# A graph network's node stage in batches of ten tiles with lagged matmuls, and the ranking's products laid out by stream

## The reference

```python
h = relu(layernorm(x))
x = x + L0(h)      # relu(LN(segment_sum((h @ W_lin @ W_gcn)[src] * norm, dst) + b_gcn) * gamma + beta)
h = relu(layernorm(x))
x = x + L1(h, edge_attr_128, edge_attr_128_n2)
# L1, four heads of 32: q = h @ Wq + bq for nodes; k, v from the two edge arrays
# score = (q[src] . k) * scale; softmax over the edges of one src; out = segment_sum(attn * v, src) @ Wo + bo
```

## Time and profile before

| | |
|---|---|
| median of 3 runs | 4865.36 us (4861.69 to 4885.93) |
| the profiled execution | 4897.3 us, span 4895.6 us |
| busy: PE, DVE, ACT, POOL | 3389.2, 2855.3, 2454.4, 2047.4 us |
| mean granted TensorE clock | 0.771 |
| moved by DMA | 764.21 MB, 156 GB/s over the span |

### The profile page before, as it was taken

One profiled execution on the slowest core, in us unless ns is written; L12 is line 12 of the kernel. 1 busy time (PEld: TensorE's weight loads), 2 busy tenths in 40 slices (PEclk: granted clock), 3 DMA queues, 4 the chain that ended last, 5 costly groups with the idle time before them and its releaser, 6 DMA issues. The chain is left out here.

```text
span 4895.6 us, 79918 instructions
## 1 busy us (share of the span) xinstructions
PE 3389.2 (69%) x21299; PEld 2441.0 (50%) x21299; DVE 2855.3 (58%) x5810; ACT 2454.4 (50%) x7415; POOL 2047.4 (42%) x1890
## 2 busy tenths in 40 slices
PE   3488767778777774021454567666668998999898
PEld 2266544455554452011333455555556776777665
DVE  6877787888887673530000455555556777777611
ACT  0545598888898784010232334333334665666411
POOL 1677287777777777777001433333331000000000
PEclk7655579999998897555555788888888999999855
DMA  1554144444444545456211566666666666666400
GB/s 59 168 173 163 49 138 162 155 160 160 161 151 157 170 160 183 142 170 208 88 33 53 187 207 222 216 208 214 212 209 196 189 190 203 189 189 190 132 0 26
DMA packets 511558, 764.21 MB, mean 156 GB/s; under 512 B 53848, under 2 KB 377408, under 8 KB 511358
## 3 DMA queue, kind: packets, MB, share of 16 engines
q1 hardware_dynamic: 406798, 522.56, 35.2%
q0 software_dynamic: 78160, 226.14, 12.2%
q10 hardware_dynamic: 26400, 13.21, 0.9%
HBM read 515.95 MB, written 245.75 MB: 156 GB/s over the span
## 5 line engine op out<-in xcount | busy, mean ns | idle before, releaser
L550 POOL DMA_INDIRECT table_s<-ring,place x1612 | 1894.3, 1175 | 1158.0 <-DMA ring<-in_kv 576.0
L623 ACT ACTIVATE row_base<-row_base 128x196 f32<-128x196 f32 x1616 | 883.3, 557 | 200.2 <-DVE row_base L718 189.5
L1346 PE MATMUL bank<-kT,G 128*128 128x384 f32 x1200 | 573.3, 562 | 235.9 <-ACT kT L1393 139.4
L1393 ACT COPY kT<-bank 128x384 f32<-128x384 f32 x600 | 286.5, 477 | 595.3 <-remote 264.6
L1366 PE MATMUL bank<-kv_rows,exT 128*128 128x129 f32 x3600 | 536.1, 288 | 0.0
L943 PE MATMUL bank<-xres 128*128 128x98 bf16 x3136 | 315.3, 236 | 291.4 <-ACT work L662 192.2
L1437 DVE TENSOR_REDUCE gmax<-bank 128x1 f32<-128x384 f32 x600 | 333.2, 555 | 299.2 <-remote 116.7
L962 PE MATMUL bank<-parts,work 128*128 128x384 bf16 x2401 | 501.2, 367 | 0.0
L1366 PEld LDWEIGHTS bank<-kv_rows,exT 128*128 128x128 f32 x3600 | 486.7, 205 | 0.1
L662 ACT CAST work<-bank 128x392 bf16<-128x392 f32 x784 | 373.1, 510 | 165.4 <-PE bank L943 98.3
L1017 DVE SCALAR_TENSOR_TENSOR others<-kv_rows,node_s,iota_h 128x384 bf16<-128x384 f32 x600 | 371.4, 619 | 135.1 <-DMA kv_rows<-table_s 79.2
(11 more groups left out here) (272 smaller groups left out, 4915.5 us busy)
## 6 DMA issues: line engine op xcount, KB each, us to landing
kv_rows<-table_s SPq DMA_DIRECT2D x600, 408.0 KB, 3.1
ring<-in_kv SPq DMA_DIRECT2D x402, 512.0 KB
G<-G_dram SPq DMA_DIRECT2D x600, 64.5 KB, 2.7
table_s<-ring,place POOLq DMA_INDIRECT x1612
G_dram<-gst ACTq DMA_DIRECT2D x50, 258.0 KB
x_dram<-xres SPq DMA_DIRECT2D x1, 3200.0 KB, 15.2
out<-ring SPq DMA_DIRECT2D x1, 3072.0 KB
table_s<-parts SPq DMA_DIRECT2D x6, 136.0 KB, 3.8
```

The source lines that it names most:

```text
L550: pool.indirect_dma_start(out=m["table_s"], out_offset=bass.IndirectOffsetOnAxis(ap=m["place"][0:n, i, k:k + 1], axis=0), in_=m["ring"][0: ...
L623: last = nc.scalar.activation(at, at, ACT.Identity, accum_out=m["place_f"][:, i % 2, h * STREAMS // 2 + k:h * STREAMS // 2 + k + 1])
L1346: pe.matmul(scores[k][:, 0:SGE], m["G"][:, u, 0:P], m["kT"][:, k, :], start=False, stop=True, skip_group_check=True).then_inc(m["scored"], 1)
```

## The change

POOL_STEPS becomes (130, 144). `scatter_rows` copies the keys of the next step before it waits for this one's places. `products` is laid out as half, stream, tile, so that VectorE writes with a stride of 196 elements and ScalarE sums over neighbours. In the node stage the norm goes in five batches of ten tiles, each in eight stages; while a batch's tiles pass through the matmuls, the next batch's stages are done between them on VectorE. The four `qm` move from ScalarE to VectorE (with the bias added before the scale, so `qbias` is gone), `hs` from VectorE to ScalarE. TensorE does the transpose two tiles ahead and the Wq product one tile ahead. `gst` has four buffers; its store is issued one tile later. All loops of the stage are written out. `x` is loaded in three DMAs, the first ten tiles at once and without a wait, and stored in five. The diff, cut:

```diff
-POOL_STEPS = (132, 156)
+POOL_STEPS = (130, 144)
+BATCH_T, GSTS = 10, 4
...
 def scatter_rows(m, pool, i):
     u, first = i % KRING, STREAMS - columns(i)
-    need(pool, m["rows_sent"][u], sent_before(i))
-    pool.tensor_copy(m["ring"][:, u, first:STREAMS, KEY_AT:KEY_AT + 1], m["sources"][:, i, first:STREAMS].rearrange("p (s a) -> p s a", a=1)).then_inc(m["keys_ready"], 1)
+    for j in ((0, 1) if i == 0 else (i + 1,) if i + 1 < STEPS else ()):
+        v, at = j % KRING, STREAMS - columns(j)
+        need(pool, m["rows_sent"][v], sent_before(j))
+        pool.tensor_copy(m["ring"][:, v, at:STREAMS, KEY_AT:KEY_AT + 1], m["sources"][:, j, at:STREAMS].rearrange("p (s a) -> p s a", a=1)).then_inc(m["keys_ready"], 1)
     pool.wait_ge(m["places_ready"], i + 1)
...
-                        at = m["products"][:, h, :, k:k + 1].rearrange("p t a -> p (t a)")
+                        at = m["products"][:, h, k, :]
...
-                    dve.tensor_tensor(m["products"][:, h, :, :].rearrange("p (b t) s -> p b t s", b=RANK_BANKS),
+                    dve.tensor_tensor(m["products"][:, h, :, :].rearrange("p s (b t) -> p b t s", b=RANK_BANKS),
...
         def _(sp):
+            for k, (first, end) in enumerate(((0, BATCH_T), (BATCH_T, N // P))):
+                sp.dma_start(m["xres"][:, first:end, :], node_tiles(m["x"][first * P:end * P, :])).then_inc(m["x_again_loaded"][k], 16)
             sp.wait_ge(m["x_padded"], 1)
-            load_x(m, sp)
+            sp.dma_start(m["xres"][0:N % P, N // P, :], m["x"][N // P * P:N, :]).then_inc(m["x_again_loaded"][1], 16)
             for i in range(POOL_STEPS[0] + KRING, POOL_STEPS[1] + KRING):
                 load_rows(m, sp, i)
-            sp.wait_ge(m["x_ready"], 1)
-            sp.dma_start(node_tiles(m["x_dram"]), m["xres"][:, :, :]).then_inc(m["x_stored"], 16)
+            for b in range(NT // BATCH_T):
+                sp.wait_ge(m["x_ready"], b + 1)
+                sp.dma_start(node_tiles(m["x_dram"])[:, part(b), :], m["xres"][:, part(b), :]).then_inc(m["x_stored"], 16)
...
+            def queries(t):
+                u = t % 2
+                dve.wait_ge(m["q_summed"], t + 1)
+                need(dve, m["G_summed"], t - 1)
+                for h in range(HEADS):
+                    last = dve.tensor_scalar(m["qm"][:, u, :, h, :], m["bank"][2 + u][:, 0:P].rearrange("d (q n) -> d q n", q=PARTS),
+                                             m["w"]["bq"][:, 0:1], m["qscale"][:, h:h + 1], ALU.add, ALU.mult)
+                last.then_inc(m["q_ready"], 1)
+            for stage in range(8):
+                normal(0, stage)
+            for t in range(NT):
+                b, stage = t // BATCH_T + 1, t % BATCH_T
+                if b < NT // BATCH_T and stage < 8:
+                    normal(b, stage)
+                queries(t)
...
+            for t in range(NT):
+                b, stage = t // BATCH_T + 1, t % BATCH_T
+                if b < NT // BATCH_T and stage in (2, 6):
+                    root(b, stage // 4)
+                if t + 3 < NT:
+                    hidden(t + 3)
+                if t + 2 < NT:
+                    turned(t + 2)
+                if t > 0:
+                    stored(t - 1)
+                taken(t)
...
+            for t in range(NT):
+                if t + 2 < NT:
+                    turn(t + 2)
+                if t + 1 < NT:
+                    query(t + 1)
+                keyed(t)
```

More of the change, by code:

```diff
@@ L1182, in nodes_block, with part @@
 def nodes_block(nc, m):
+    def part(b):
+        return slice(b * BATCH_T, (b + 1) * BATCH_T)
     with nc.Block() as block:
@@ L1252, in _, with root, hidden @@
-            rounds(act, copies, 0, NT // 2, 2)
-            for u in range(2):
-                act.wait_ge(m["G_stored"][u], NT // 2 * 16)
+            def root(b, which):
+                act.wait_ge(m["sqrt_asked"], 2 + 2 * b + which)
+                nc.scalar.activation(m["std"][:, part(b)], m["var"][:, part(b)], ACT.Sqrt).then_inc(m["sqrt_done"], 1)
+            def hidden(t):
+                if t % BATCH_T == 0:
+                    act.wait_ge(m["norm_ready"], 3 + 2 * (t // BATCH_T))
+                need(act, m["h2_transposed"], t - 1)
+                nc.scalar.activation(m["hs"][:, t % 2, :], m["work"][:, t, :], ACT.Relu, scale=m["rstd"][:, t:t + 1]).then_inc(m["h2_ready"], 1)
@@ new lines, in stored @@
+            def stored(t):
+                act.wait_ge(m["G_ready"], t + 1)
+                act.dma_start(m["G_dram"][t * PARTS * P:(t + 1) * PARTS * P, :].rearrange("(q d) n -> d q n", q=PARTS),
+                              m["gst"][:, t % GSTS, :, :]).then_inc(m["G_stored"][t % GSTS], 16)
+            for which in range(2):
+                root(0, which)
+            hidden(0)
+            hidden(1)
+            turned(0)
+            hidden(2)
+            turned(1)
+            for t in range(NT):
[9 more added lines that the diff above has]
+                taken(t)
@@ L1256, in _, with turn @@
+            stored(NT - 1)
+            for v in range(GSTS):
+                act.wait_ge(m["G_stored"][v], len(range(v, NT, GSTS)) * 16)
         @block.tensor
         def _(pe):
-            def body(i, u, r):
-                pe.wait_ge(m["h2_ready"], i + 1)
-                need(pe, m["h2T_ready"], i - 1)
-                pe.transpose(m["bank"][u][:, 0:P], m["hs"][:, u, :], m["ident"][:, :]).then_inc(m["h2_transposed"], 1)
-                pe.wait_ge(m["h2T_ready"], i + 1)
-                need(pe, m["q_ready"], i - 1)
-                pe.matmul(m["bank"][2 + u][:, 0:P], m["w"]["Wq"][:, :], m["hT"][:, u, :], start=True, stop=True).then_inc(m["q_summed"], 1)
-                pe.wait_ge(m["q_ready"], i + 1)
-                need(pe, m["G_ready"], i - 1)
+            def turn(t):
+                pe.wait_ge(m["h2_ready"], t + 1)
+                need(pe, m["h2T_ready"], t - 1)
+                pe.transpose(m["bank"][t % 2][:, 0:P], m["hs"][:, t % 2, :], m["ident"][:, :]).then_inc(m["h2_transposed"], 1)
@@ L1271, in body @@
                 last.then_inc(m["G_summed"], 1)
-            rounds(pe, body, 0, NT // 2, 2)
+            turn(0)
+            turn(1)
+            query(0)
+            for t in range(NT):
[4 more added lines that the diff above has]
+                keyed(t)
 def layer1_block(nc, m):
@@ L1614, in gnn_kernel @@
             for name, shape, dt in (
-                    *((n, [P, NT], F32) for n in small), ("flags_i", [P, 1], I32), ("qscale", [P, HEADS], F32), ("qbias", [P, HEADS], F32),
+                    *((n, [P, NT], F32) for n in small), ("flags_i", [P, 1], I32), ("qscale", [P, HEADS], F32),
                     ("hs", [P, 2, D], F32), ("work", [P, NT, D], F32), ("acc", [P, NT, D], F32), ("xres", [P, NT, D], F32)):
@@ L1712, in gnn_kernel @@
                 general_block(nc, m)
-            for name, shape, dt in (("qm", [P, 2, PARTS, HEADS, SN], F32), ("gst", [P, 2, PARTS, P + 1], F32)):
+            for name, shape, dt in (("qm", [P, 2, PARTS, HEADS, SN], F32), ("gst", [P, GSTS, PARTS, P + 1], F32)):
                 m[name] = place(front, name, shape, dt)
```

121 lines of the change are left out of this document (66 added, 55 removed).

## The result

The changed kernel took 4881.92 us (median of 20 runs, 4778.88 to 5006.74), the kernel before 4872.8 (20 runs, 4861.21 to 4921.27): no gain to speak of. The forecast was 4492, 4430 to 4635. The profiled execution took 4857.05 us with a span of 4855.3, where the sum said 4524: 333 too little.

What follows compares the result with a forecast made beforehand. POOL was taken to end the scatter block, with engines taking turns within node-stage tiles. Scatter block -62, node stage -415 and layer 1 +104 made -373: profiled 4897.3 to 4524, median 4492 us, range 4430 to 4635.

Steps and rivals of the forecast that it cites:

- Products, stream by stream: Ranking: ScalarE's sums about 0.1 us faster each but off the path, VectorE's strided write 0 dearer; total unchanged.
- the third rival: Ranking: VectorE's strided write costs double or more, so VectorE ends the block; 5242 at three times; chance 0.04, 0.02 for no change.
- The prediction's own sign of being wrong: Ranking: VectorE's product L718 above 1.1 us with the ranking past 1945 would show the forecast wrong.
- The stall as one of the loops: Node stage and layer 1: gaps come from loops beside POOL's scatter; written-out code is free of them.
- Node stage: Batched norm, lagged matmuls and written-out loops: 240 us instead of 656, 415 saved (ends 340 and 435).
- Layer 1: Starts with 58 scatter steps left instead of 46: 12 x 8.7 = 104 us dearer (ends 80 and 115).
- Keys ahead: Scatter block: copying keys early saves POOL 0.5 us in each of 102 steps, 51 of the block's 62 us.
- POOL as the bound: Node stage: POOL needs 23 us a step, 337 us in all, total about 4585; chance 0.10, shared with a hand-over bound.
- Stalls stay: Node stage: the 30 us a tile come from the scatter, not loops; 360 us instead of 240, total 4612; chance 0.15.

Runs made afterwards that it cites:

- keys ahead: The kernel before with only the next step's keys copied ahead by POOL: 4407.96 us beside 4471.9 for the kernel before (0.985); a second time 4409.04 (0.986).

## Why the prediction was wrong

**Products, stream by stream** is the first step that failed. It took VectorE's strided write at 0 because L340 reads 800 bytes apart at 1.04 ns an element (833 ns for 808 is 1.03). That row has one source and a jump on the read; the product has two sources, and at a jump on either side it takes 1562 to 1630 ns for 784 elements, 2.0 to 2.1 ns each, where 968 is 1.23. Priced in time, the layout costs 184 us alone and 175 us inside the change, where the sum had 0. The dearer write stood in the prediction, as the third rival with 0.06, and the rule quoted from the Trainium skill, "SBUF — State Buffer", Door 1, was right about the write and about ScalarE's gain; this case's runs agree with 968 against 1562 ns and 557 against 355. L340's row shows no such price, and I let this row of another form outweigh the rule. The rival's way was not the one seen on a calm chip, though: it had VectorE end the block instead of POOL, beyond 34 us of slack. The instruction took 0.594 us more and not under 0.1, yet POOL still ended the block, 170 us later. On the chip of the result VectorE did end it, narrowly, with its last L819 at 2286.63 and POOL's last scatter at 2279.98, but there the gaps had held it up too. The prediction's own sign of being wrong, L718 above 1.1 us with the ranking past 1945, is in the trace. ScalarE's sum, forecast at 455 ns, fell to 355; it lies off the path, as said.

**The stall as one of the loops** is the second. The step set gaps in loops beside a scattering POOL against a ranking written out without loops, and took the ranking as free of them. Its own rows say less than that: the earlier trace rows has 21.87 us remote before L830, which is written out, and in the whole ranking of before VectorE stood 73 us and ScalarE 33 us remote, in waits of up to 21.9 and 6.5 us. The gaps there were shorter, not absent. Two of the kernels break the rule outright: gaps of 86 us in written-out code (the changed kernel), and loops beside a scattering POOL without any (keys ahead, calm chip). The second no row could have shown, since all came from one chip. What the runs show in the rule's place: the gaps are there or not by the chip and the time, and they are waits for late updates of TensorE's semaphores. What varied between my places was POOL's pace as well as the code's form, and I weighed only the form. The share of the miss can't be split exactly: on a calm chip the layout is worth 170 us of the block's end, and 342 was missed here; but the change without it, on a gapped chip, missed the block's end by 377.

**What held.** *Node stage*: 254 us, forecast 240, and 241 on a calm chip. Of its 402 us 265 are saved on a calm chip too (506 - 241), by the norm in batches, the lag and, for 22, the written-out code; the other 137 are gaps, so the forecast's 415 was right on the chip it was made for and 150 too much for a calm one. The four other traces from gapped chips have it at 252 and 298 us with 14 steps and 300 and 333 with 19. POOL's steps in it took 12.1 us, forecast 14.4. *Layer 1*: +82, forecast +104 with ends 80 and 115; on a calm chip +30, because a round there takes 17.9 us beside POOL instead of 23.7, and 15.3 without it, and (17.9 - 15.3) x 12 = 31. The 8.7 us a round were gaps for the most part: the waits of layer 1 have ScalarE's `kT` at 46.1 us remote in 200 us after, as in the earlier trace rows, and nothing remote on a calm chip.

```profile
ACT kT L1467 <- remote: 46.1, 7, 8.0
```

*Keys ahead*: the copy was forecast at -51 of the block's -62 and measured -64 in the whole time; the gap between copy and scatter fell to 0.16 us, not 0.30, and the step from 10.85 to 10.2. *POOL as the bound*, a rival: no, it stood 80.28 us before its last task of the node stage. *Stalls stay*, in the node stage: hardly, in the trace of the result (the longest remote wait is 9.6 us); in three of the other four traces from gapped chips one of about 30 us stood there, and the rival's 360 us were reached in none. The place where the gaps did stay, and grew, was the ranking, which no case of mine had.

**The parts on a calm chip** add up, as measured: keys ahead -64, node stage -265 and layer 1 +30 make -299, and the change without its layout measured -298 and -300. That confirms the parts, not the forecast: its own terms made -373 for the same three, with the node stage 150 too large and layer 1 74 too dear, two errors that partly cancel there. On the chip of the forecast even the right price for the layout would have given 4492 + 175 = 4667 and not 4882.

## What to carry to other kernels

A layout has a price on both of its sides: move it from the engine with room to the one that is 80% busy and it must be measured on an instruction of the same form, with as many sources, before a row of another form may set it to zero. For a gap that the trace puts down to something remote, look up which semaphore the line waits for and when its last raiser ended; here that names TensorE. And such a gap belongs first to the chip on which it was taken: take a profile of the unchanged kernel on a second one before building a forecast on the gap or a kernel around it. And a part of a change that pays on one chip (the keys copied ahead, 64 us on a calm one) has to be tried by itself on the kind of chip that the kernel is to run on.

## What the runs showed of the hardware

- Remote waits of up to 86.1 us on VectorE and 57.9 on ScalarE, and idle times of TensorE of up to 66.0 us, stood in the traces of two of seven sets and in those of the forecast and the result, only while POOL issued indirect transfers, and in none of the other five sets. The kernel before is 10% slower there (4904 and 4915 against 4468).
- In these traces updates of semaphores that TensorE raises are recorded late: 303 in the kernel before and 334 in the changed one over 1 us behind the matmul, the latest 67.5 us. In the 14 traces from calm chips none is; the median there is 0.014 us. Why they come late is open.
- A product of 784 f32 elements from a bank and a bf16 one-hot takes 968 ns where all three sides go in runs of 4, 1562 with a write 784 bytes apart, and 1608 with reads 32 and 16 bytes apart. ScalarE's sum over 196 elements takes 557 ns at a step of 16 bytes and 355 side by side.
- Where VectorE's product is longer, POOL's indirect DMAs are too: 1237 ns instead of 1155 in the mean over 1612, for the change with and without its layout in one set on a calm chip. The slower product thus comes with a slower scatter, and there the scatter sets the block's end.
